# Waits of GpSimd for recent gathers taken out of the two edge stages of a graph network kernel

## The reference

```python
# layer 0: attention over the edges, 4 heads of 64
h = (x @ W).reshape(N, H, C)
e = leaky_relu(a_src[src] + a_dst[dst], 0.2)
e_exp = exp(e - e_max[dst])
alpha = e_exp / (segment_sum(e_exp, dst, N)[dst] + 1e-16)
out = segment_sum(h[src] * alpha[:, :, None], dst, N)
# layer 1: products of rows with weights made from the edge's attributes
w = silu(edge_scalars @ fc_w1 * c) @ fc_w2 * c2        # 4 x 64 per edge
xg0, xg1 = y0[edge_src], y1[edge_src]                  # 64 and 64 x 3
mids = concat(w_a*xg0*ea0, w_b*einsum(xg1, ea1), (w_c*xg0)*ea1, (w_d*ea0)*xg1)
agg = segment_sum(mids, edge_dst, N)
```

## Time and profile before

| | us |
|---|---|
| timed runs, median of 3 | 3763.07 (3760.01 to 3765.9) |
| profiled execution, first to last instruction (span) | 3834.3 |
| edge stage 0, first gather to last sum | 110.9 to 1446 |
| edge stage 1, first gather to last group of VectorE begun | 2044.2 to 3441.7 |
| TensorE busy, whole span | 3096.8 (81%) |
| VectorE busy | 2264.0 (59%) |
| GpSimd busy | 1887.1 (49%) |
| granted TensorE clock, mean | 0.884 |

### The profile page before, as it was taken

How to read it: one execution, slowest core, us unless ns; L and a number is a source line. 1 busy time by engine, 2 the same in 40 slices (tenths; PEclk the granted TensorE clock), 3 DMA queues, 4 the chain that set the end, 5 groups by cost and what they waited for, 6 DMA issues and landing times. The chain is left out here.

```text
span 3834.3 us, 80836 instructions
## 1 busy us (share of the span) xinstructions
PE 3096.8 (81%) x22728; PEld 2335.4 (61%) x22728; DVE 2264.0 (59%) x6165; ACT 1426.5 (37%) x4367; POOL 1887.1 (49%) x2266
## 2 busy tenths in 40 slices
PE   6577777777777768789996888888888888878499
PEld 4466666666666666578884545555554545548388
DVE  5455565555555557756665656566666656666712
ACT  5122222222222216623332444454444544417322
POOL 3566666666666641111114566666665555541144
PEclk9788888888888889999997989898889998989699
DMA  6433333333333336533223333333333323325321
GB/s 194 125 93 89 92 92 90 92 91 90 92 90 94 97 89 179 167 98 91 83 75 94 89 88 91 90 91 92 91 90 90 87 80 88 97 75 170 113 53 48
DMA packets 239108, 375.94 MB, mean 98 GB/s; under 512 B 88190, under 2 KB 145606, under 8 KB 238762
## 3 DMA queue, kind: packets, MB, share of 16 engines
q0 software_dynamic: 89712, 230.26, 21.7%
q1 hardware_dynamic: 147482, 140.83, 13.2%
q10 hardware_dynamic: 1696, 2.62, 0.2%
HBM read 310.75 MB, written 62.84 MB: 97 GB/s over the span
## 5 line engine op out<-in xcount | busy, mean ns | idle before, releaser
L1990 POOL DMA_INDIRECT e_rows<-tab,e_ix x828 | 785.3, 948 | 447.1 <-issue 333.0
L588 POOL DMA_INDIRECT e_rows<-tab,e_ix x830 | 789.1, 951 | 345.2 <-issue 302.8
L983 PE MATMUL e_pU<-e_ohp,e_rows 128*128 128x128 f32 x3340 | 516.0, 321 | 17.6 <-issue 13.6
L983 PEld LDWEIGHTS e_pU<-e_ohp,e_rows 128*128 128x128 f32 x3340 | 499.9, 237 | 26.9 <-issue 21.0
L2232 PE MATMUL e_pU<-e_msg,e_oh 128*32 128x128 f32 (+1 forms) x6672 | 427.9, 326 | 40.8 <-issue 34.8
L2162 DVE TENSOR_TENSOR e_msg<-e_pW,e_rows 128x256 f32<-128x256 f32 x417 | 176.5, 423 | 457.9 <-remote 251.5
L2164 DVE TENSOR_TENSOR e_msg<-e_pW,e_rows 128x384 f32<-128x384 f32 x834 | 422.2, 548 | 0.0
L697 ACT CAST e_ohT<-e_pT 64x640 bf16<-64x640 f32 x167 | 114.4, 685 | 825.1 <-remote 451.3
L2218 PE MATMUL e_pW<-e_w,e_hT 64*128 64x256 f32 x1668 | 340.9, 459 | 71.8 <-DVE e_msg L2164 24.3
L2232 PEld LDWEIGHTS e_pU<-e_msg,e_oh 128*32 128x32 f32 x6672 | 263.0, 117 | 194.0 <-issue 135.4
L964 PE MATMUL e_pT<-ident,e_oh 128*64 128x128 f32 x835 | 152.1, 321 | 185.5 <-issue 95.4
(11 more groups left out here) (453 smaller groups left out, 5669.7 us busy)
## 6 DMA issues: line engine op xcount, KB each, us to landing
e_rows<-tab,e_ix POOLq DMA_INDIRECT x1658
xnT<-f_xnT SPq DMA_DIRECT2D x25, 250.0 KB, 3.0
e_xk<-xnT SPq DMA_DIRECT2D x25, 250.0 KB
xnT<-b_xT SPq DMA_DIRECT2D x25, 250.0 KB, 2.9
m_xnT<-xnT SPq DMA_DIRECT2D x25, 250.0 KB
xnT<-m_xT SPq DMA_DIRECT2D x25, 250.0 KB, 2.7
ffn_norm<-xnT SPq DMA_DIRECT2D x25, 250.0 KB
tab<-f_hrow SPq DMA_DIRECT2D x25, 227.5 KB
```

The source lines that it names most:

```text
L588: nc.gpsimd.indirect_dma_start(out=rows[:, s, j, :], out_offset=None, in_=env["tab0"], in_offset=bass.IndirectOffsetOnAxis(ap=at[:, j:j + ...
L983: nc.tensor.matmul(pU[:, s % 2, 2 * W * k:2 * W * (k + 1)], rows[:, s, j, 128 * k:128 * k + 128], ohp[:, s % 3, j, 2 * k:2 * k + 2, :], st ...
L1990: nc.gpsimd.indirect_dma_start(out=rows[:, r % PER, j, :], out_offset=None, in_=env["tab1"], in_offset=bass.IndirectOffsetOnAxis(ap=at[:, ...
```

## The change

In both edge stages three conditional waits of GpSimd go. In stage 0 the one before the index copy, for the second gather (`s_row[1]`) of the group being issued. In stage 1 the same, and the one before the first gather of a group, for the fifth gather (`s_row[T1 - 2]`, T1 - 2 = 4) of the last group. The order of gathers and copies, all other waits, and the other engines' instructions stay. Each wait is followed by a nop, which goes too.

```diff
--- before.py
+++ after.py
@@ edges0, GpSimd
                             if lo >= 1:
                                 for i in ((j,) if j < 3 else range(3, GT) if j == 3 else ()):
                                     hold(pool, s_row[i], 16 * g)
-                            if j == 3:
-                                hold(pool, s_row[1], 16 * (g + 1))
                             if j == 3 and hi <= GROUPS - 2:
                                 nc.gpsimd.tensor_copy(ix[:, (s + 1) % 2, :], srcI[:, bass.ds((g + 1) * GT, GT)])\
                                   .then_inc(s_ix, 1)
@@ edges1, GpSimd
                             if lo >= 1:
                                 for i in ((j,) if j < 3 else range(3, T1) if j == 3 else ()):
                                     hold(pool, s_row[i], 16 * g)
-                            if j == 3:
-                                hold(pool, s_row[1], 16 * (g + 1))
-                            elif j == 0 and lo >= 1:
-                                hold(pool, s_row[T1 - 2], 16 * g)
                             if j == 3 and hi <= GROUPS1 - 2:
                                 nc.gpsimd.tensor_copy(ix[:, (r + 1) % 2, :], srcI[:, bass.ds((g + 1) * T1, T1)])\
                                   .then_inc(s_ix, 1)
```

## The result

| | before | after |
|---|---|---|
| timed beside each other, median | 3761.54 (3752.89 to 3765.9, 4 runs) | 3344.60 (3342.83 to 3347.88, 4 runs) |
| profiled span | 3834.3 | 3344.2 |
| edge stage 0 | 110.9 to 1446 | 110 to 1198 |
| edge stage 1 | 2044.2 to 3441.7 | 1795 to 2954 |
| granted TensorE clock, mean | 0.884 | 0.925 |

The ratio is 0.8898, with a 95% interval from 0.8886 to 0.8909: 11% faster, where 0.3% was forecast. Rival (d), which the prediction had excluded, came nearest with 3435 us.

A forecast was written before the change was run, and what follows sets the result against it. The ring of TensorE, ScalarE and VectorE was taken to bound nearly all of both edge stages, GpSimd only their beginnings. Gains of 5 us (stage 0) and 8 us (stage 1) took 3763 to 3750 us, range 3737 to 3768.

The forecast's parts named there:

- (d): Both edge stages: GpSimd is the bound after all, nearly 330 us would go, 3435 us; excluded by the readers' lag.
- Who holds whom: Both edge stages: whether GpSimd or its readers set the pace; answered as the consumers, except at the stages' beginnings.
- The counts do: Gathers issued against groups read: VectorE about two groups behind in stage 0, four in stage 1, so rows lie landed.
- The waits agree: VectorE's waits: in stage 0 after 160 us, 11.8 us for rows against 229.9 us "remote"; GpSimd waits for its readers.
- Scaled by that the 13 us change by 0.2: Whole kernel: profiled span 71 us, 1.9%, above the timed median; judged too small to alter the 13 us gain.
- What the waits cost GpSimd: Both stages: 193 us idle before the index copies and about 135 us before stage 1 groups no longer forced.
- What it is worth: Gain only at the stages' starts: 5 us in stage 0 and 8 us in stage 1.
- the tests named: Profile signs: copy idle 0.3 us or less, gathers 0.95, slot waits grow, later paces stay 7.8 and 10.1 us.
- The rule weighed: GpSimd locked out by VectorE's two-port mode, gathers lengthening and gain 0 instead of -13; no chance worth a number.
- (b): Edge loops: closer gathers lengthen TensorE's gaps if these are instruction code arriving by DMA; 35 us more, 3785 us, chance 0.10.

The follow-up runs named there:

- gapped: Sets of runs in which the kernel before took 3809 to 3830 us and TensorE stands idle between products with nothing visible ending it.
- f1: The kernel before, unchanged, profiled a second time: 3740.82 us, span 3739.1.
- plain: Sets of runs in which the kernel before took 3743 to 3762 us, its TensorE traces without such idle gaps beyond a few.
- h1: The kernel after, unchanged, run once more in another set: 4308.04 us beside 3819.67 for before, ratio 1.1287.
- k2: The kernel after with a GpSimd memset in each of the three places of the waits, beside a before of 3808.81 us: 4092.74 us.
- k1: The kernel after with each gather reading rows of a quarter of the width, beside a before of 3808.81 us: 4303.37 us.
- l1: The kernel after with only three gathers a group in both stages, beside a before of 3830.24 us: 3323.09 us.
- l2: The kernel after with only one gather a group in both stages, beside a before of 3830.24 us: 3232.52 us.
- f2: The kernel before with a GpSimd memset added before each index copy of stage 0, behind the wait: 3798.42 us beside 3744.87.
- e3: The kernel after with a GpSimd memset of 760 columns in each of the three places of the waits: 3526.51 us beside 3742.76 for before.

## Why the prediction was wrong

**Who holds whom** was the step that failed. "The counts do" and "The waits agree" were read rightly from their trace, but the trace was of a gapped execution, and the timed runs were not. In f1, the same code, the ring is nearly empty and 302.7 us go for rows in stage 0. The lag on which (d) was "excluded" exists, for this kernel, in the gapped kind alone.

**"Scaled by that the 13 us change by 0.2"** was the moment to stop. The profiled span was 71 us above the median, when the timed runs themselves lay within 6 us. The two stages took 1335 + 1397 = 2732 us in the profile; f1 has 1284 + 1357 = 2641, measured alike, and a span shorter by 95. Nearly the whole surplus, 92 us, sat in the two stages that were to be predicted. The prediction's own rows could have warned. Its 7.2 and 9.4 us left out that the gather behind the copy starts after 0.50 us and not 0.30; with that and the mean idle of 0.84 GpSimd's chain is 7.5 and 9.7 us, or 167 x 7.5 + 139 x 9.7 = 2601 us. If the 71 us were missing from the stages, the timed runs spent 2732 - 71 = 2661 us there, within 60 us of that chain.

**What the waits cost GpSimd** was right in kind and short in size: 193 + 135 = 328 us were put at the three waits. The floor of the gap before the copy is 0 and not 0.2, and the gather behind it starts 0.34 us sooner, so stage 0 frees 1.2 us a group instead of 0.64. A free group takes 6.37 us (forecast 6.6). In stage 1 it would take 7.6 (forecast 7.8), but the consumers stop it at 8.5, so 198 us come out of it where 87 + 135 = 222 had been put at its waits.

**What it is worth**: 5 and 8 us were forecast; the stages of after are 195 and 198 us shorter than those of f1, and it was in every group, not at the starts. Of the tests named, the idle before the copies (0) and the gathers' length (950 ns) came true; that the paces stay at 7.8 and 10.1 did not, and GpSimd's waits for slots grew in stage 1 only, to 83.7 us.

**The rule weighed** (that denser gathers meet VectorE and get longer) changed nothing, as the text had it: 952 and 950 ns after, against 951 and 948. The section of the Trainium skill (SBUF — State Buffer, SBUF: two separate sides) gives its 620 and 3100 ns for a DMA issued by GpSimd, not for a gather; no run here shows whether VectorE was ever in such a mode, so the rule is not tested by these numbers.

**The rivals.** (d) had the mechanism of the plain sets. Its 3435 us was 90 too high: in stage 0 it had 107 us for the 195 that went, by the 0.34 us behind the copy and the floor of 0.2; in stage 1 it had 24 too many; and the last 20 lie between the sets, since before took 3762 us beside after and 3741 in f1. (b) had a part of what the gapped sets show, TensorE's gaps growing under denser gathers, with 22 us instead of the 488 measured. That they come of the gathers' bytes on the DMA engines is refuted by the quarter of bytes; that they are instruction code is neither shown nor excluded. Both readings were worth having; the chances of 0 and 0.10 came from a trace that was taken for typical.

## What to carry to other kernels

When the profiled execution is longer than the timed runs by more than these differ among themselves, compute each stage's pace and ask where the surplus lies before reading waits: if it lies in the stage of the change, the profile may show another bottleneck than the timed runs have. Where the engine's own chain (here 7.5 us of 7.53) equals the pace of the stage, a lag of the reader by some groups doesn't clear it; a second profile does. A wait for a recent transfer in the issuing engine's stream costs what is left of its flight in every group, where that engine's chain sets the pace, so wait for the buffer or the index that is needed and nothing younger, and time such a change in several sets, on more than one chip, before it is kept.

## What the runs showed of the hardware

TensorE can lose up to 2.65 us (h1, line 971 at 1323.90) between products with no wait between them while GpSimd issues gathers: some 408 gaps of over 0.2 us (255 us) in the middle of stage 1 of h1, 73 with more pauses between the gathers (k2), 395 with a quarter of the bytes (k1), 49 with three gathers a group (l1). With one a group (l2) there was none, but that run may have been a plain one. The same two programs differ by -11% in one set and +13% in another. A gather occupies GpSimd for 0.95 us whether it moves 260 or 65 floats a row (953 ns with the narrow ones). And behind a copy that had to wait for a transfer the next gather starts 0.50 us later, behind one that had not 0.16 us (f1 and f2; the same in after and e3).
